# A 1-core macaron stack: the order of the picked experts' last outputs, table making, storing by chunk, and a first layer in halves

## The reference

```python
# layer 0, feed-forward: a small net steers cycles of mixing (3 cycles a call, 2 calls)
h = gelu(h @ w1 + b1)          # 128 -> 128, the "first layer"
h = gelu(h @ w2 + b2)          # 128 -> 64
h = gelu(h @ w3 + b3)          # 64 -> 32
gate = sigmoid(h @ w4 + b4)    # 32 -> 1
...
# layer 3
x = x + 0.5 * _L3_ffn_ref(_layernorm(x), ...)     # first call ("t1_")
x = x + _L3_attn_ref(_layernorm(x), ...)          # global ("g"), then local ("l") attention
x = x + 0.5 * _L3_ffn_ref(_layernorm(x), ...)     # second call ("t2_"), the end of the program

def _L3_ffn_ref(x, Wg, W1, W2, W3, Ws1, Ws2, Ws3):    # 32 experts of 64, the best 4 of each token
    weights, indices = top_k(softmax(x @ Wg), 4)
    for e in range(32):
        y[tok] += (silu(xg @ W1[e]) * (xg @ W3[e])) @ W2[e] * w
    return y + (silu(x @ Ws1) * (x @ Ws3)) @ Ws2      # and a shared expert of 128

def _L3_attn_ref(...):         # x = rmsnorm(x), q and k are turned by cos/sin tables (rope), q/k norm
    x = x + global_latent_attn(rmsnorm(x, norm1_w), ...)
    x = x + local_gqa_attn(rmsnorm(x, norm2_w), ...)
```

## Time and profile before

| | us |
|---|---|
| median of 3 runs | 1764.86 |
| lowest, highest | 1763.65, 1768.14 |
| the profiled execution, whole | 1765.89 |
| its span in the trace | 1764.1 |
| TensorE busy in it | 1602.2 (91%) |
| VectorE busy in it | 962.3 (55%) |
| ScalarE busy in it | 799.1 (45%) |

### The profile page before, as it was taken

One profiled execution on the slowest core, in us unless ns is written; L12 is line 12 of the kernel. 1 busy time (PEld: TensorE's weight loads), 2 busy tenths in 40 slices (PEclk: granted clock), 3 DMA queues, 4 the chain that ended last, 5 costly groups with the idle time before them and its releaser, 6 DMA issues. The chain is left out here.

```text
span 1764.1 us, 34453 instructions
## 1 busy us (share of the span) xinstructions
PE 1602.2 (91%) x13581; PEld 917.2 (52%) x13585; DVE 962.3 (55%) x2183; ACT 799.1 (45%) x1306; POOL 357.2 (20%) x501
## 2 busy tenths in 40 slices
PE   7979978899998997999799989999699987979998
PEld 2436644455554664445544555666434444745665
DVE  7673347988872334544563344445744436763445
ACT  5643323576765332442234333221588865643221
POOL 1315222232322523301330023000500100132000
PEclk9989988899998998999799999999899988989999
DMA  4632116111103211000000004553321004316554
GB/s 109 241 109 89 49 48 166 49 55 33 57 4 136 86 45 43 1 1 1 1 0 1 1 32 106 116 128 83 84 81 40 19 19 115 102 32 135 114 114 96
DMA packets 56258, 120.84 MB, mean 68 GB/s; under 512 B 8439, under 2 KB 35095, under 8 KB 51299
## 3 DMA queue, kind: packets, MB, share of 16 engines
q1 hardware_dynamic: 53628, 113.55, 24.0%
q0 software_dynamic: 2432, 5.00, 0.8%
q10 hardware_dynamic: 39, 0.07, 0.0%
HBM read 85.38 MB, written 19.96 MB: 60 GB/s over the span
## 5 line engine op out<-in xcount | busy, mean ns | idle before, releaser
L2479 DVE TENSOR_REDUCE a_most<-psum 128x1 f32<-128x512 f32 (+3 forms) x304 | 180.7, 655 | 37.7 <-PE psum L2109 36.8
L2437 ACT ACTIVATE a_probs<-psum 128x512 f32<-128x512 f32 (+1 forms) x304 | 153.6, 583 | 83.8 <-PE psum L2109 82.2
L3349 ACT ACTIVATE t_silu<-psum 128x512 f32<-128x512 f32 x136 | 81.2, 597 | 240.7 <-PE psum L3407 239.6
L3424 PEld LDWEIGHTS psum<-t_slot,t_hid 128*128 128x128 f32 x1024 | 132.1, 191 | 55.9 <-issue 49.8
L3520 DVE TENSOR_TENSOR t_prod<-t_silu,psum 128x512 f32<-128x512 f32 x104 | 71.5, 687 | 137.4 <-ACT t_silu L3349 137.4
L2740 ACT ACTIVATE ga_probs<-psum 128x1024 f32<-128x1024 f32 (+2 forms) x160 | 137.1, 953 | 19.7 <-PE psum L2109 19.2
L3424 PE MATMUL psum<-t_slot,t_hid 128*128 128x128 f32 x1024 | 134.4, 276 | 2.9 <-DVE t_hid L3511 2.9
L3407 PE MATMUL psum<-xnT,t_slot 128*128 128x512 f32 x256 | 131.2, 594 | 3.1 <-ACT t_silu L3349 3.1
L3412 PE MATMUL psum<-xnT,t_slot 128*128 128x512 f32 x256 | 130.7, 592 | 0.0
L2109 PE MATMUL psum<-a_ks,a_qs 96*32 96x512 bf16 (+3 forms) x1536 | 123.3, 341 | 4.6 <-DVE a_most L2479 2.5
L2109 PE MATMUL psum<-a_qs,a_ks 128*32 128x512 bf16 (+3 forms) x1536 | 116.1, 328 | 5.0 <-DMA a_qs<-a_most_parts 2.0
(11 more groups left out here) (453 smaller groups left out, 3012.7 us busy)
## 6 DMA issues: line engine op xcount, KB each, us to landing
t_spread<-factors SPq DMA_DIRECT2D x64, 512.0 KB, 6.4
m_experts<-experts_dram SPq DMA_DIRECT2D x14, 768.0 KB, 9.2
c_halves<-xnT SPq DMA_DIRECT2D x48, 128.0 KB, 2.3
t_slot<-experts_dram SPq DMA_DIRECT2D x32, 192.0 KB, 5.2
a_qs<-scratch_q SPq DMA_DIRECT2D x16, 288.0 KB
a_ks<-scratch_k SPq DMA_DIRECT2D x24, 192.0 KB
ga_qs<-scratch_q SPq DMA_DIRECT2D x16, 288.0 KB
la_qs<-scratch_q SPq DMA_DIRECT2D x16, 288.0 KB
```

The costliest lines, as they stand in the source:

```text
L2437: act.activation(probs[:, (n * BLOCKS + b) % PROBS, h0:h0 + heads, 0:wide], src, ACT.Exp, scale=SCALE).then_inc(probs_ready, 1)
L2479: v.tensor_reduce(most[:, row, h0:h0 + heads, qt % KPH], src, AX.X, ALU.max).then_inc(max_read, 1)
L3349: act.activation(silu[:, n % 2, :], core.psum[:, g_bank(n), :], ACT.Silu).then_inc(silu_ready, 1)
L3424: ins = pe.matmul(core.psum[:, c, t * P:(t + 1) * P], left[:, t * P:(t + 1) * P], weights, start=pair < 0 and t == 0, stop=False, skip_gro ...
```

## The change

- `top4_stage`: the last eight steps (BY_CHUNK = 60 on) go by chunk: pairs 14 and 15 of chunk 0, then of chunk 1, and so on, so that a chunk's sum is complete every second step. `downs_before(n)` says how many outputs stand ahead of `up(n)`: as before up to n = 43; from n = 44 to 60 every second step has one more, so that the lag falls from 12 to 3. VectorE's list keeps two `weigh` ahead of that count (`weighed < downs_before(n) + 2`), each behind `multiply(n)`, until n = 59; from 60 on `weigh(n - 1)` stands ahead of `multiply(n)`. x of chunk c is added inside, between the last steps.
- First call: statistics and normalisation of chunks 0 and 1 for the "g" attention (`Ahead`, `NORMED = 2`) stand between the last steps too, and ScalarE makes the tables of both attentions (class `TurnTable`) after its last silu.
- Second call: each chunk of x is stored as soon as it is added, in four DMAs; `last_stage` only waits for the weight loads.
- `gqa_project_stage`: no tables; in "g" only chunks 2 and 3 have statistics and normalisation, chunk 3's behind the first `join`, and the first chunk is turned before the joined weights are finished.
- `front_stage`: layer 1 is two matmuls of 64 weight columns each, at array columns 0 and 64.

```diff
@@ front_stage, layer1 @@
-                pe.matmul(core.psum[:, p, :], w("cn_w1"), out(p), start=True, stop=True).then_inc(l1_out, 1)
+                for r in (0, HALF):
+                    cols = slice(r, r + HALF)
+                    ins = pe.matmul(core.psum[cols, p, :], w("cn_w1")[:, cols], out(p), start=True, stop=True, tile_position=(0, r), skip_group_check=True)
+                ins.then_inc(l1_out, 1)
@@ top4_stage @@
+    BY_CHUNK, LAST_LAG = STEPS - 2 * NC, 3
+    CATCH_UP = BY_CHUNK - 2 * (LAG - LAST_LAG)
+    NORMED = 2
...
     def pair_of(n):
-        return n // NC - 1
+        return n // NC - 1 if n < BY_CHUNK else PAIRS - 2 + (n - BY_CHUNK) % 2
+
+    def chunk_of(n):
+        return n % NC if n < BY_CHUNK else (n - BY_CHUNK) // 2
+
+    def downs_before(n):
+        extra = min(max(n - CATCH_UP, 0) // 2, LAG - LAST_LAG)
+        return min(n - LAG + 1 + extra, STEPS)
...
@@ SyncE @@
+            if dram_out is not None:
...
+                for c in range(NC):
+                    sp.wait_ge(added, c + 1)
+                    sp.dma_start(out[:, TPC * c:TPC * (c + 1), :], core.x[:, TPC * c:TPC * (c + 1), :]).then_inc(stored, 16)
+                sp.wait_ge(stored, 16 * NC)
@@ ScalarE @@
             for n in range(TURN, STEPS):
                 evacuate(n)
+            if last_work is not None:
+                last_work(act, wide_made)
@@ TensorE @@
+            done = NC
             for n in range(EARLY, STEPS):
-                down(n - LAG)
+                while done < downs_before(n):
+                    down(done)
+                    done += 1
                 up(n)
-            for n in range(STEPS - LAG, STEPS):
+            for n in range(done, STEPS):
                 down(n)
@@ VectorE @@
-            for n in range(EARLY, STEPS):
+            weighed = NC + 2
+            for n in range(EARLY, BY_CHUNK):
                 multiply(n)
-                if n + 2 - LAG < STEPS:
-                    weigh(n + 2 - LAG)
-            for n in range(STEPS + 2 - LAG, STEPS):
-                weigh(n)
-            for c in range(NC):
...
+                while weighed < downs_before(n) + 2:
+                    weigh(weighed)
+                    weighed += 1
+            for n in range(BY_CHUNK, STEPS):
+                for m in range(weighed, n):
+                    weigh(m)
+                weighed = n
+                c, odd = divmod(n - BY_CHUNK - 2 * 2, 2)
+                if c >= 0 and not odd:
+                    add(c)
+                    statistics(c)
+                if c >= 0 and odd and following:
+                    following.normalise(v, c)
+                multiply(n)
+            weigh(STEPS - 1)
+            add(NC - 2)
+            add(NC - 1)
@@ gqa_project_stage, ScalarE @@
                 act.activation(joined[:, 0:D], w("g_q"), ACT.Copy).then_inc(joined_ready, 1)
+                ln.scalar(act, 0, gain=gain)
...
-            act.activation(turn_by[:, :, :, :].rearrange("p f k (d h) -> p (f k d) h", h=GROUP), by_tile, ACT.Copy).then_inc(turn_by_ready, 1)
...
-            ln.scalar(act, 0, gain=gain)
+            if kind == "l":
+                ln.scalar(act, 0, gain=gain)
@@ gqa_project_stage, VectorE @@
-            ln.vector(v)
-            v.wait_ge(table_ready, 2)
+            for c in range(ln.ahead, NC):
+                ln.statistics(v, c)
+            for c in range(ln.ahead, NC - 1):
+                ln.normalise(v, c)
...
             both_products(0)
             join(0)
+            ln.normalise(v, NC - 1)
```

More of the change, by code:

```diff
@@ L253, in pool @@
         g.wait_ge(self.var_ready, b)
[L254 removed]
+        var, eps = k.meanvar[:, a:b, 1], self.eps
         if self.rms_eps:
@@ L3288, in top4_stage @@
         down_pe = core.sem(ctx, tag + "down_pe")
+        added = core.sem(ctx, tag + "added")
+        following = norm(ctx) if norm else None
+        if dram_out is not None:
+            stored = core.sem(ctx, tag + "stored")
+        if last_work is not None:
+            wide_made = core.sem(ctx, tag + "wide_made")
         block = core.block(ctx)
@@ L3311, in _ @@
                 g.tensor_tensor(prod[:, n % PRODS, :], silu[:, n % 2, :], upper[:, n % 2, :], ALU.mult).then_inc(early_ready, 1)
+            if following:
+                for c in range(NORMED):
+                    following.pool(g, c)
         @block.sync
@@ L3414, in down @@
             def down(n):
-                c, pair = n % NC, pair_of(n)
+                c, pair = chunk_of(n), pair_of(n)
                 if pair < 0:
@@ L3504, in weigh @@
             def weigh(n):
-                pair, c = pair_of(n), n % NC
+                pair, c = pair_of(n), chunk_of(n)
                 if c == 0:
@@ L3520, in multiply, with add, statistics @@
                 v.tensor_tensor(prod[:, n % PRODS, :], silu[:, n % 2, :], core.psum[:, u_bank(n), :], ALU.mult).then_inc(prod_ready, 1)
+            def add(c):
+                v.wait_ge(down_pe, BY_CHUNK + 2 * c + 2)
+                xs = core.x[:, TPC * c:TPC * (c + 1), :].rearrange("p t d -> p (t d)")
+                v.scalar_tensor_tensor(xs, core.psum[:, c, :], 0.5, xs, ALU.mult, ALU.add).then_inc(added, 1)
+            def statistics(c):
+                if following:
+                    v.wait_ge(added, c + 1)
+                    following.statistics(v, c)
@@ new lines, in _, with __init__, scalar @@
+            weigh(STEPS - 1)
+            add(NC - 2)
+            add(NC - 1)
+RMS_EPS = 1e-6
+class TurnTable:
+    TILES, KV = T // P, 4
+    QK = D + KV * HD
+    HN = QK // HD
+    def __init__(self, core, ctx, tag, w5, kind):
+        self.src = w5[:, L3_COLS[kind + "cos"][0]:L3_COLS[kind + "cos"][0] + 2 * self.TILES * HD]
+        self.turn_by = core.sb(ctx, tag + "turn_by", [P, 2, self.TILES, HD * GROUP])
+        self.table = core.sb(ctx, tag + "table", [P, self.TILES, 2, self.QK])
+    def scalar(self, act, wide_made, nth):
+        wide, n = self.turn_by, 2 * self.TILES * HD
+        by_tile = self.src.unsqueeze(2).broadcast_to([P, n, GROUP])
+        act.activation(wide[:, :, :, :].rearrange("p f k (d h) -> p (f k d) h", h=GROUP), by_tile, ACT.Copy).then_inc(wide_made, 1)
+        act.wait_ge(wide_made, nth)
+        for f in range(2):
+            dst = self.table[:, :, f, :].rearrange("p k (g r) -> p k g r", r=HD * GROUP)
+            act.activation(dst, wide[:, f, :, :].unsqueeze(2).broadcast_to([P, self.TILES, self.HN // GROUP, HD * GROUP]), ACT.Copy)
@@ L3541, in gqa_project_stage @@
+def gqa_project_stage(core, w5, w5_in, table, v_all, stacks, xr, kind, tag):
     nc = core.nc
@@ L3920, in build @@
                 stacks = Stacks(core, actx, tag, sems[tag], scratch3, (P, 2 * 4 * HD), [T], ring, 1, pair=2)
-                gqa_project_stage(core, w5, w5_in, v_all, stacks, xr, kind, kind + "p_")
+                gqa_project_stage(core, w5, w5_in, tables[kind].table, v_all, stacks, xr, kind, kind + "p_")
                 if kind == "g":
```

52 lines of the change are left out of this document (25 added, 27 removed).

## The result

The changed kernel takes 1799.22 us (median of 4 runs, 1798.39 to 1801.71) against 1764.34 for the kernel before on the same chip (1763.65 to 1768.14): ratio 1.0196, 95% interval 1.0174 to 1.0217. That is 34.9 us slower, inside the range, and 6.8 more than the 1792.4 that was predicted.

The account below looks back on a forecast made before the run. TensorE bounds the picked experts' steady part; an output whose scaling stands behind the product starts 1.59 us late. Terms 19.1 + 14.4 - 2.5 - 1.8 - 1.7 = +27.5 on 1764.86 gave 1792.4 us, range 1783 to 1802.

Parts of the forecast that it names:

- The catch-up (+27.0 a call): Picked experts, steps 44 to 60: moved outputs wait for their scaling, making each call 27.0 us later.
- rival C: TensorE's clock falls to 1.2 GHz in steps 44 to 60: about 6.9 us a step, total 1815 to 1884; 8%.
- 4.21 for a step: Time of each of the seventeen steps 44 to 60, single or double output, instead of 2.62 us.
- Rival A: In steps 44 to 60 outputs find their inputs already scaled: no waiting, -10.3 us, total 1754.6; 4%.
- rival B: In steps 44 to 60 only double-output steps wait, 0.69 us each: +2.1, total 1767.0, no measurable change; 4%.
- The second call (+14.4): Picked experts' second call: 27.0 us later from steps 44 to 60, less 12.6 at its end: +14.4 us.
- T: The moment at which `up(n)` has gone through TensorE; at a call's end, n = 67.
- The first call (+19.1): Picked experts' first call: 27.0 us later, less (14.0 - 6.1) at its end, where ScalarE's tables finish last: +19.1 us.
- "g" (-2.5): Opening of the "g" attention stage: projection starts after 3.5 to 3.7 us against 6.2; -2.5 us, bounds -1 and -6.
- the bound's own reason (-6): Opening of the "g" attention: TensorE rests about 3 us instead of nearly 4 and might keep its clock; -6 us.
- "l" (-1.8): Opening of the "l" attention stage: projection starts at about 1451.3 instead of 1453.16; -1.8 us, bounds -1 and -3.
- The front (-1.7): Front stage, layer 1 in halves: three changes of shape a cycle go, over six cycles; -1.7 us, bounds -3 and +2.

Follow-up runs that it names:

- Experiments 1 and 2: Changed kernel with `weigh` ahead of `multiply` in steps 43 to 59: 1757.26 us; changed kernel with three `t_hid` buffers, scaling three ahead, order kept: 1756.56 us.

## Why the prediction was right, and where it was off

**The catch-up (+27.0 a call): right, 2.0 too small.** Every sign asked for is there: steps 4.3 apart, L3458 released by L3548 with a short and a long wait by turns, and PEclk 1.00 (busy 75.55 of 92.00 us in both calls' stretches), so not rival C. The mis-sized term is 4.21 for a step: it measured 4.32, since an output that has waited takes 0.99 and not 0.90. 17 x 0.1 is about 2 a call. Experiments 1 and 2 show the cause. Rival A describes what the kernel does once it is mended, not what it did; rival B's single step without a wait is in no trace.

**The second call (+14.4): +16.2.** Span end at T + 8.0 (said: T + 8.2); the rest is the 2.0.

**The first call (+19.1): +22.7.** The tail was right: ScalarE's tables end at T + 5.9 (6.1), x at T + 4.8 (5.0), the stage 6.8 behind T. On top come the 2.0, and 1.7 for the first scaled output, 2.63 - 0.92. This last was no part of the sum; in the table it goes with placement (see the end of this section).

**"g" (-2.5): -5.5.** Projecting began 2.1 us into the stage and not 3.5. Two terms were mis-sized. The first turning took not 1.24 as before but 0.60, at full clock, which was the bound's own reason (-6); and from the evacuation's end (1261.97) to the first projection (1262.63) it took 0.66 and not 1.3, since two of the small copies were made ahead of that evacuation. The prediction named this sign. The opening gives 4.1 of the 5.5; where the other 1.4 comes from wasn't looked into. **"l" (-1.8): -2.8**, inside its bounds.

**The front (-1.7): -2.5 in these two traces, but about -1 in all.** The starts of the next stage lie at 123.6 to 125.2 with whole layers (four kernels, mean 124.3) and at 121.6 to 123.7 with halves (five kernels, mean 123.0); the two kernels with empty instructions, left out here, have 122.3 whole and 124.8 in halves. In a cycle two halves follow in the same shape:

```profile
39.63 1.03 PE L671 MATMUL psum<-c_hid,w 128*64 128x512 f32 x4
40.49 1.03 PE L664 MATMUL psum<-xnT,w 128*64 128x512 f32 x4
41.48 1.07 PE L679 MATMUL psum<-c_hid,w 128*64 128x512 f32 x2
42.31 1.10 PE L671 MATMUL psum<-c_hid,w 128*64 128x512 f32 x4
```

From L671 to L671 these take 2.68; before, 41.89 to 44.81 took 2.92. Two changes of shape are gone, and halves cost no more: two products take 1.94 (L664 x8), whole ones 1.98. The Trainium skill, TensorEngine Tiling (Array Packing), Tiling Modes, has the drain at a change of mode, and the trace agrees. The Trainium skill, TensorE: Matmul & The Clock Gate, Part 3, whose 2.38 for three tiles would have cost +2.7 here, is not borne out for two halves (1.94 against 1.98).

**What no step held: +7.2 in an attention that nobody touched.** The prediction took everything outside the edits for unchanged. The experiments show that the number of real instructions ahead of it decides, with 256 as good as none. DMA queues of the changed kernel, 421 to 424 us:

```profile
q8 instruction: 1, 0.02, 2.2%
```

This 16 KB packet of the instruction queue is under way from 421.90 to 422.94, and the wait lasts from 421.99 to 424.32. There are 33 such packets from 335 to 530 us, one in 6 us, and 111 in the whole span, to TensorE's 27166 recorded instructions in the kernel before (13581 products, 13585 weight loads), some 245 a packet: the queue is TensorE's. After five of the 33 TensorE waits, and each of the five waits ends 1.3 to 1.5 us behind the packet's landing; in the other kernels all 25 waits of this kind over 0.3 us end 1.3 to 1.7 us behind one. I read this as TensorE waiting for its instructions. Which instruction must stand where for a packet to be late wasn't tried, and the place isn't all: the changed kernel with a whole layer 1 has one such wait of 1.3 where the kernel before has none. The Trainium skill, Runtime: NRT & Kernel Launch, Instruction fetch mechanics, has instructions fetched in blocks of 16 KiB, 256 of them, mostly hidden. The block's size agrees with the period found; the hiding holds for 28 of the 33 packets here, and not for the five with waits of up to 2.3 us.

The first scaled output's 1.7 us go with the same packets. The copy of the factors (`t_spread`) is issued at 1077.38 before and at 1078.86 in the changed kernel, and the first scaling starts 7.2 us behind it before, 8.6 now. In between one instruction packet lands now and none before. DMA queues of the changed kernel, 1078.86 to 1087.43 us (before, 1077.38 to 1084.61 has no such row):

```profile
q8 instruction: 1, 0.02, 0.9%
```

So it is in all fourteen kernels' traces: the six moved by 96 have one packet of 1.0 to 1.3 us there, and scale 8.3 to 8.8 us behind the issue; the eight others have none, and scale after 7.0 to 7.5. That the packet holds the factors up is my reading of this; it wasn't tried by an experiment. The scaling then ends 0.54 to 0.56 us behind the end of the GpSimd product that it meets, in all fourteen (1085.62 against 1085.08 before, 1088.81 against 1088.26 now). These products are 1.71 us apart, in step with gate and up, and a scaling that comes 1.2 us later meets the next one: so the wait is 0.92 or 2.63, 1.71 more, and in no kernel anything between.

What stays open is the clock's earlier return (-3.1, which by luck made up for part of the attention). So the close total rests in part on two errors of opposite sign.

## What to carry to other kernels

When a consumer is moved forward in one engine's list, its producer's place in the other list has to move too, or there must be a buffer more: an engine that is idle half the time is no help if the idle time lies ahead of an instruction that waits in order. Read off the trace how long behind the releasing event a producer finishes, and multiply by the steps in which it has nothing made ahead. And where a stage of many small products follows, compare its length also when only earlier code has changed: here 96 instructions cost 9 us in two places, and adding 160 more gave it back.

## What the runs showed of the hardware

- The first attention, whose code is the same in all kernels, took 262 to 265 us with 0 real instructions added to TensorE's list ahead of it, 263 to 264 with 256, 266 with 160 and 269 to 272 with 96. 96 empty instructions (`pe.nop`) left it at 262, and 160 of them beside the 96 real ones at 269.
- TensorE's waits for nothing shown in that attention end 1.3 to 1.7 us behind the landing of a 16 KB packet of the instruction queue.
- A scaling on VectorE that takes 0.68 us alone took 0.71 to 1.66 beside a GpSimd product, and ended 0.54 to 0.56 us behind it.
- A product of a 32x32 tile with 4 columns is cheap: 80 matmuls in 2.69 us, 34 ns each with their weight loads, against 12.34 us for 80 of 128x128 with 8 columns, of which part ran at 1.2 GHz.
- TensorE's granted clock fell from 2.4 to 1.2 GHz during 12.3 us of back-to-back products of 8 columns, in which the profile shows it busy throughout.
- An output of eight matmuls takes 0.99 us after a wait and 0.90 without.
